# Cross attention of a decoder: the softmax denominators as matmuls of ones over every tile of exps, instead of adds on GpSimd and VectorE ahead of them

## What is computed

```python
xn = layernorm(x, ...)                      # the context, 64 keys a batch, 192 wide
ln = layernorm(latents, ...)                # the 1024 tokens themselves, 256 wide
q  = ln @ Wq.T
kv = concatenate([xn @ Wkv.T, ln @ Wlkv.T], axis=1)
...                                         # 4 heads of 64; q and k normed per head
attn = where(full_mask, qn @ kn.T, -max)
attn = softmax(attn, axis=-1)               # over 1024 + 64 keys
out  = (attn @ v) -> (b, 1024, 256)
return out @ Wo.T + bo
```

## Time and profile before

| | |
|---|---|
| median of 3 runs | 1945.41 us (1944.75 to 1947.19) |
| the profiled execution | 1944.75 us, span 1943.0 us |
| busy over the span | TensorE 1688.1 us (87%), VectorE 941.2 (48%), ScalarE 625.1 (32%), GpSimd 119.4 (6%) |
| loop of the cross attention | about 423 to 700 us of the span |
| exps of the slots (line 878) | 64, 65.5 us |
| values (line 747), exps by v | 69.5 us busy |

### The profile page before, as it was taken

How to read it: one execution, slowest core, us unless ns; L and a number is a source line. 1 busy time by engine, 2 the same in 40 slices (tenths; PEclk the granted TensorE clock), 3 DMA queues, 4 the chain that set the end, 5 groups by cost and what they waited for, 6 DMA issues and landing times. The chain is left out here.

```text
span 1943.0 us, 19762 instructions
## 1 busy us (share of the span) xinstructions
PE 1688.1 (87%) x7458; PEld 955.6 (49%) x7458; DVE 941.2 (48%) x1490; ACT 625.1 (32%) x1024; POOL 119.4 (6%) x92
## 2 busy tenths in 40 slices
PE   5796795989999958977799999778767999999998
PEld 3443442543222213333444544345553888888886
DVE  3404404567656541133587775355545536353542
ACT  2312322432232231114166666242242222221220
POOL 0000000001121200003500000000011000000000
PEclk8898897989999979988899999899968999999999
DMA  4001000000000000002724520000111022222211
GB/s 174 0 0 59 0 0 4 0 1 1 1 1 1 1 1 0 0 0 76 87 82 52 67 34 2 3 1 0 52 36 58 1 87 87 87 87 87 87 30 44
DMA packets 27693, 67.47 MB, mean 35 GB/s; under 512 B 3096, under 2 KB 14424, under 8 KB 25176
## 3 DMA queue, kind: packets, MB, share of 16 engines
q1 hardware_dynamic: 27608, 66.33, 12.5%
HBM read 57.80 MB, written 8.39 MB: 34 GB/s over the span
## 5 line engine op out<-in xcount | busy, mean ns | idle before, releaser
L1566 ACT ACTIVATE arena<-psum 128x512 f32<-128x512 f32 (+3 forms) x384 | 164.3, 499 | 123.6 <-PE psum L1470 91.6
L1606 DVE TENSOR_REDUCE b_mx<-psum 128x1 f32<-128x512 f32 (+3 forms) x304 | 181.5, 653 | 45.0 <-PE psum L1448 34.4
L2100 PE MATMUL psum<-m_wo,m_hidden 128*128 128x256 f32 (+1 forms) x704 | 153.4, 379 | 1.0 <-DVE arena L2303 1.0
L2198 ACT ACTIVATE m_gelu<-psum 128x512 f32<-128x512 f32 (+1 forms) x88 | 52.6, 598 | 305.1 <-PE psum L2086 305.1
L2100 PEld LDWEIGHTS psum<-m_wo,m_hidden 128*128 128x128 f32 (+1 forms) x704 | 133.3, 190 | 19.7 <-issue 1.2
L2086 PE MATMUL psum<-m_x_high,m_w_high 128*128 128x512 f32 (+1 forms) x352 | 139.9, 398 | 2.9 <-issue 2.9
L2086 PE MATMUL psum<-m_x_rest,m_w_high 128*128 128x512 f32 (+1 forms) x352 | 138.8, 394 | 0.0
L2086 PE MATMUL psum<-m_x_high,m_w_rest 128*128 128x512 f32 (+1 forms) x352 | 138.4, 393 | 0.0
L2322 DVE TENSOR_TENSOR m_hidden<-m_gelu,psum 128x512 f32<-128x512 f32 (+1 forms) x88 | 60.5, 688 | 139.8 <-PE psum L2086 139.8
L878 ACT ACTIVATE x_probs<-psum 128x1024 f32<-128x1024 f32 x64 | 65.5, 1024 | 179.4 <-PE psum L734 179.4
L954 DVE TENSOR_REDUCE x_mx<-psum 128x2 f32<-128x1024 f32 x64 | 77.4, 1222 | 83.6 <-PE psum L708 82.4
(11 more groups left out here) (372 smaller groups left out, 2730.8 us busy)
## 6 DMA issues: line engine op xcount, KB each, us to landing
m_w<-w SPq DMA_DIRECT2D x16, 1368.0 KB, 8.9
m_wo<-wo SPq DMA_DIRECT2D x8, 1280.0 KB
weights_sb<-weights SPq DMA_DIRECT2D x2, 2820.0 KB, 8.9
b_q_stack<-b_q_dram SPq DMA_DIRECT2D x36, 128.0 KB, 6.9
b_k_stack<-b_k_dram SPq DMA_DIRECT2D x36, 128.0 KB, 7.4
weights_sb<-weights SPq DMA_DIRECT2D x1, 3328.0 KB, 13.0
b_q_dram<-b_q_parts SPq DMA_DIRECT2D x6, 512.0 KB, 3.3
b_k_dram<-b_k_parts SPq DMA_DIRECT2D x6, 512.0 KB, 4.4
```

What stands on the lines that cost most here:

```text
L1566: act.activation(probs[slot % RING][:, 0:n], score(slot)[:, 0:n], ACT.Exp, scale=SCALE).then_inc(s["expd"].sem)
L1606: dve.tensor_reduce(mx[:, part, qi, heads[0]:heads[0] + nh], tile(("piece", p))[:, 0:nh * keys].rearrange("p (h n) -> p h n", n=keys), AX, ...
L2100: mm = pe.matmul(bank[:, q * D:(q + 1) * D], hidden[0:H_N(h), h, (2 * i + q) * P:(2 * i + q + 1) * P], wo[0:H_N(h), h, :], start=(h == 0), ...
```

## The change

The adds on GpSimd and VectorE go, with `pool_sum`, `dve_sum` and `add_up`. TensorE sums each tile of exps itself: after `values` of the slots `kt` 1, 3, 5 and 7 it issues four matmuls with ones of 128x32 as stationary operand, two tiles by two heads, each into its own group of 32 partitions of `den_tile`; after `values` of slot 8 two more with 64 rows. The four groups hold partial sums (two for each head). `copy_out` now copies both banks (`psum[2]`, output and partial sums) to an `x_out` twice as wide. In slot 2 of the next step `spread_den` multiplies the copied partial sums by the constant `spread`, which has ones in four of its rows and so adds the two partial sums of a head and spreads them over its 64 rows. That result takes a place in the shared ring, from which `normalise` (now in slot 2 instead of 3) takes the reciprocal. `project` and `finish` move from slot 7 to slot 6. `exps` now waits only for the values (and the sums with them) that still read the tile.

```diff
+            if n >= 1 and kt == 2:
+                order.append(("den", n - 1))
-            if n >= 1 and kt == 7 and part_of(n - 1)[2] == FT - 1:
+            if n >= 1 and kt == 6 and part_of(n - 1)[2] == FT - 1:
                 order.append(("project", n - 1))
...
-    order.append(("project", STEPS - 1))
+    order += [("den", STEPS - 1), ("project", STEPS - 1)]
...
-        ones = sb("x_ones", [P, DH])
+        spread = sb("x_spread", [P, P])
+        ones = sb("x_ones", [P, 32])
...
-        out_sb = sb("x_out", [P, CH])
-        pool_sum = [sb(f"x_pool_sum{i}", [P, PAIR, CH]) for i in range(2)]
-        dve_sum = sb("x_dve_sum", [P, PAIR, CH])
+        out_sb = sb("x_out", [P, 2 * CH])
...
+                pool.memset(spread[:], 0.0)
...
-                for n in range(STEPS):
-                    if n >= 2:
-                        pool.wait_ge(*s["den"](n - 1))
-                    for kt in range(1, POOLED):
-                        slot = GROUPS * n + kt
-                        pool.wait_ge(*s["expd"](slot + 1))
-                        if kt > 1:
-                            pool.wait_ge(*s["pooled"]((POOLED - 1) * n + kt - 1))
-                        pool.tensor_tensor(pool_sum[n % 2][:], probs[(slot - 1) % RING][:] if kt == 1 else pool_sum[n % 2][:],
-                                           probs[slot % RING][:], ALU.add).then_inc(s["pooled"].sem)
+                pool.wait_ge(g["zeroed"].sem, 3)
+                pool.memset(spread[0:1, 0:DH], 1.0)
+                pool.memset(spread[32:33, DH:P], 1.0)
+                pool.memset(spread[64:65, 0:DH], 1.0)
+                pool.memset(spread[96:97, DH:P], 1.0).then_inc(g["consts"].sem)
...
+                    if kt % 2 == 1:
+                        for back in (1, 0):
+                            for h in range(PAIR):
+                                group = PAIR * (1 - back) + h
+                                mm = pe.matmul(den_tile[group * 32:(group + 1) * 32, :], ones[:], probs[(slot - back) % RING][:, h, :],
+                                               start=(kt == 1), stop=(back == 0 and kt == TT - 1))
+                    if kt == TT:
+                        for h in range(PAIR):
+                            mm = pe.matmul(den_tile[h * 32:(h + 1) * 32, :], ones[0:KEYS, :], probs[slot % RING][0:KEYS, h, :],
+                                           start=False, stop=True)
                     mm.then_inc(s["av"].sem)
 
-                def add_up(n):
-                    pe.wait_ge(*s["pooled"]((POOLED - 1) * (n + 1)))
-                    pe.wait_ge(*s["added"]((TT - POOLED) * (n + 1)))
-                    if n >= 1:
-                        pe.wait_ge(*s["den_inv"](n))
-                    for i, of in enumerate((pool_sum[n % 2], dve_sum)):
-                        for h in range(PAIR):
-                            mm = pe.matmul(den_tile[h * DH:(h + 1) * DH, :], ones[:], of[:, h, :], start=(i == 0), stop=(i == 1))
-                    mm.then_inc(s["den"].sem)
+                def spread_den(n):
+                    to = tile(("den", n))
+                    pe.wait_ge(*s["out_copied"](n + 1))
+                    pe.matmul(to[:, 0:CH], spread[:], out_sb[:, CH:2 * CH], start=True, stop=True).then_inc(s["made"].sem)
...
-                        m, of = divmod(slot - RING, GROUPS)
-                        act.wait_ge(*s["av"](slot - RING + 1))
-                        if of < POOLED:
-                            act.wait_ge(*s["pooled"]((POOLED - 1) * m + max(of, 1)))
-                        else:
-                            act.wait_ge(*s["added"]((TT - POOLED) * m + max(of - POOLED, 1)))
+                        act.wait_ge(*s["av"](slot - RING + 1 + (1 if (slot - RING) % GROUPS % 2 == 0 and (slot - RING) % GROUPS < TT else 0)))
...
-                    act.activation(out_sb[:], out_tile, ACT.Copy).then_inc(s["out_copied"].sem)
+                    act.activation(out_sb[:], c.psum[2][:], ACT.Copy).then_inc(s["out_copied"].sem)
...
-                def add(slot):
...
                 def normalise(n):
                     b, half, m = part_of(n)
-                    dve.wait_ge(*s["den"](n + 1))
-                    dve.reciprocal(den_inv[:], den_tile).then_inc(s["den_inv"].sem)
-                    dve.wait_ge(*s["den_inv"](n + 1))
-                    dve.wait_ge(*s["out_copied"](n + 1))
-                    dve.tensor_tensor(ot[b][:, m, half * CH:(half + 1) * CH], out_sb[:], den_inv[:], ALU.mult).then_inc(s["normed"].sem)
+                    dve.reciprocal(den_inv[:], tile(("den", n))[:, 0:CH]).then_inc(s["read"].sem)
+                    dve.wait_ge(*s["read"](nth["den", n] + 1))
+                    dve.tensor_tensor(ot[b][:, m, half * CH:(half + 1) * CH], out_sb[:, 0:CH], den_inv[:], ALU.mult).then_inc(s["normed"].sem)
...
-                        if n >= 1 and kt == 0:
-                            add(GROUPS * n - 1)
-                        if kt > POOLED + 1:
-                            add(GROUPS * n + kt - 1)
-                        if n >= 1 and kt == 3:
+                        if n >= 1 and kt == 2:
                             normalise(n - 1)
```

More of the change, by code:

```diff
@@ L570, in cross_attention_layer @@
                                        made=0, read=0, masked=0, ctx_max=0, negated=0, max_step=0, parts=0,
-                                       scored=0, expd=0, av=0, pooled=0, added=0, den=0, out_copied=0, den_inv=0, normed=0))
+                                       scored=0, expd=0, av=0, out_copied=0, den_inv=0, normed=0))
         g = signals(nc, ctx, "xc", dict(load=1, zeroed=1, consts=1, mean=1, cent=1, sq=1, var=1, log=1, rstd=1, scaled=1,
@@ L614, in cross_attention_layer @@
         units, out_tile, den_tile = c.psum[0], c.bank(4), c.bank(5)
-        POOLED = 4
         two_heads = lambda ap: ap.rearrange("p (h n) -> p h n", h=PAIR)
@@ L640, in _ @@
                 pool.memset(same_head[0:DH, 0:DH], 1.0 / DH)
-                pool.memset(same_head[DH:P, DH:P], 1.0 / DH).then_inc(g["consts"].sem)
-                for n in range(STEPS):
-                    if n >= 2:
-                        pool.wait_ge(*s["den"](n - 1))
-                    for kt in range(1, POOLED):
-                        slot = GROUPS * n + kt
-                        pool.wait_ge(*s["expd"](slot + 1))
-                        if kt > 1:
-                            pool.wait_ge(*s["pooled"]((POOLED - 1) * n + kt - 1))
-                        pool.tensor_tensor(pool_sum[n % 2][:], probs[(slot - 1) % RING][:] if kt == 1 else pool_sum[n % 2][:],
-                                           probs[slot % RING][:], ALU.add).then_inc(s["pooled"].sem)
+                pool.memset(same_head[DH:P, DH:P], 1.0 / DH).then_inc(g["zeroed"].sem)
+                pool.wait_ge(g["zeroed"].sem, 3)
[3 more added lines that the diff above has]
+                pool.memset(spread[96:97, DH:P], 1.0).then_inc(g["consts"].sem)
             @block.tensor
@@ L831, in _ @@
                     if n >= 1 and kt == 2:
-                        add_up(n - 1)
-                    if n >= 1 and kt == 7 and part_of(n - 1)[2] == FT - 1:
+                        spread_den(n - 1)
+                    if n >= 1 and kt == 6 and part_of(n - 1)[2] == FT - 1:
                         project(n - 1)
@@ L841, in _ @@
                 values(SLOTS - 1)
-                add_up(STEPS - 1)
+                spread_den(STEPS - 1)
                 project(STEPS - 1)
@@ L1089, in _ @@
                             keep_shift(n + 1)
-                add(SLOTS - 1)
                 normalise(STEPS - 1)
```

## The result

The changed kernel takes 1981.72 us (median of 4 runs, 1981.13 to 1983.76), the kernel before 1946.24 beside it: +35.5 us, ratio 1.0185 with a 95% interval of 1.0167 to 1.0203. The profiled execution took 1980.98, its span 1979.3.

The account below looks back on a forecast made before the run. TensorE bounds the stage (busy 32.16 of 33.00 us). Rounds +32.3, last step's slots +0.8, +0.3 and +2.3, spread -4.0, copy +3.0, wait -1.3, tail +1.1: +34.5, so 1979.5 us; range 1974 to 1987.

Parts of the forecast that it names:

- The round: Each burst of sum matmuls after values, 5 per step, 40 in all: 0.95 us each, bounds 0.86 and 1.01.
- Spread for `add_up`: Slot 2: `add_up`'s 1.72 us go, one spread matmul of 1.05 comes; -0.67 a step, -4.0 in steps 1 to 6.
- The copy: Output copy twice as wide, 1.02 us for 0.59, on TensorE's path: +0.43 seven times, +3.0 us.
- The covered wait: Where steps meet, TensorE's two shift-copy waits go, with the add gone and the round after values 7 covering: -1.3 us.
- The move of the projection: Projection from slot 7 to 6, its inputs ready before it and its VectorE reader moving too: costs nothing.
- The clock: TensorE's granted clock: no term in the sum; extra or missing falls at the borders put at 1.6 us each.
- The tail: From the start of the last values 8 to the projection: 8.57 us instead of 7.51, +1.1.
- A: Rival: clock falls behind the 1.27 us copy wait at each step's start, six times, +9.6 us, 1989; chance 0.14.
- B: Rival: the four column groups run two and two, a round is 1.72 us, +31 us, 2010; chance 0.03.
- C: Rival: rounds cost TensorE nothing, -2.9 us, 1942.5; faster only below 0.07 us a round; chance 0.03 together with D.
- D: Rival: whole kernel within 0.2% (3.9 us), needing rounds of at most 0.17 us; chance 0.03 together with C.
- E: Rival: VectorE lags and piece 5 waits the whole reciprocal for its ring place, 7 x 3.4 = +24 us, 2003; chance 0.03.

Follow-up runs that it names:

- wide copy: Kernel before with only its output copy widened to 1024 columns; 1949.16 us, ratio 1.0010 to the kernel before, stage +4.1 us.
- one pair: Kernel before with copy early, VectorE's chain starting from GpSimd's sum (one add more), so one pair of sum matmuls instead of two; 1935.05 us, ratio 0.9943.
- 64-wide kernel: Changed kernel with 128x64 sum matmuls in two column groups instead of four, without the spread matmul; 1996.55 us, ratio 1.0259 to the kernel before.
- copy early: Output copy moved ahead of slot 1's exp: changed kernel 1968.95 us (ratio 1.0115), kernel before 1934.37 us (0.9941).
- rounds twice: Changed kernel with the rounds after values 3, 5 and 7 issued two times; 2005.90 us, ratio 1.0303 to the kernel before.
- before, no adds: Kernel before without any adds on GpSimd and VectorE, the sum tiles holding constants; 1943.48 us, ratio 0.9985 to the kernel before.
- after, fewer rounds: Changed kernel without the rounds after values 3, 5 and 7; 1958.83 us, ratio 1.0073 to the kernel before.

## Why the prediction was right

**The bound.** That the stage is TensorE's and that the adds stand on almost nobody's path held: without any adds the kernel gains about 2 us. What was put on TensorE came out at the end, but for the 0.2 us a slot that the last step had idle.

**The round**, the main term, was 0.99 instead of 0.95, inside the bounds 0.86 and 1.01. By the lengths of the slots that is +1.2 over the 40 rounds: slots 4 and 6 grew by 0.99, slot 0 by 0.98, slot 8 by 0.96, and the last step's slots 4 and 6 by 0.81 for 0.77. The row that described it best was the upper bound, a pair alone in its shape: a round is always alone in its shape.

**Spread for `add_up`** was 1.06 for 1.05 and right. **The copy** was right, +0.43 seven times, and is confirmed alone by the wide copy. **The covered wait** was right at 1.3, but its reason was half wrong: the add that went was enough, the round had no part in it. Another 0.5 us of small waits went with the adds, 0.4 of it in slot 6 of step 0; the sum has no term for them.

**The move of the projection**, which I put at nothing, costs 0.2 three times. Slot 7 without pieces has an idle moment in which TensorE waits for the exp. Before, the projection stood in that slot in every other step and hid it. Now it stands in slot 6, as the timeline shows:

```profile
603.03 3.70 PE L768 MATMUL psum<-weights_sb 128*128 128x512 f32 x8
606.66 1.08 PE L743 MATMUL psum<-x_probs,arena 128*64 128x512 f32 x4
...
608.98 1.13 PE L730 MATMUL psum<-arena 64*128 64x512 f32 x4
610.04 1.08 PE L743 MATMUL psum<-x_probs,arena 128*64 128x512 f32 x4
611.24 0.40 PE L725 MATMUL psum<-x_shift_t,x_ones 2*64 2x512 bf16 x2
```

From the start of slot 7's values to the next instruction it is 1.20 us (610.04 to 611.24) where a covered pair takes 1.01. That is most of why the steps that follow each other here grew by 4.6 and 4.9 us in turn (output copy to output copy: 34.94 to 39.82 with a projection, 31.56 to 36.20 without).

**The clock** was left out of the sum, rightly on the whole and luckily in one place. The fall in the last step of the earlier trace rows did not come back, -1.6. So the stage's +34.3 against a forecast of +34.5 is closer than the terms were: +1.2 for the rounds and +0.6 for the projection were missing, and -1.6 for that fall and -0.5 for the small waits made up for them. Such a near hit is luck; that the time lies between the bounds for rounds of 0.86 and 1.01 is not.

**The tail** was +1.1 and right.

**The rivals.** A (the clock falls behind the wait of 1.27) did not happen here: in five executions with six such waits each it fell behind none of the 30. But it was near: behind the one wait of 1.57 us (one pair) it fell, and at 2.19 us three times of six. B is ruled out by the bursts themselves and by the 64-wide kernel. C and D would have needed rounds of 0.07 and 0.17 us. E (the ring) did not happen: no piece waits for the reciprocal.

**Total.** The rest of the 35.5 us between the medians is not in the stage. In the profiled executions 2.1 us lie ahead of it, in code that is the same; the prediction had nothing for that. It does not come with the change: the burst of 5.84 us took 3.70 in the changed kernel with the copy early, and 5.63 in the kernel before with the copy early. Why it takes the one time or the other no run shows.

## What to carry to other kernels

Before work is taken off an engine, ask which wait of the bound engine ends on it. Here GpSimd and VectorE did 95 us of adds under TensorE's cover, and taking all of them away is worth about 2 us, while summing on TensorE costs 40 times about 1 us. The same reading pointed to what could be won: the one wait of the bound engine that came back in every step was for a copy of 0.59 us that stood behind an exp in its queue, and moving it by one place gained 8.7 us in the stage (12 in the median, ratio 0.9941), a quarter of what the whole change cost there. And a burst of matmuls that is alone in its tile shape is priced as such, not as one more of a row.

## What the runs showed of the hardware

- Four 128x32 matmuls of 512 fp32 columns in four column groups cost 0.86 us together (the second round of rounds twice), as much as two of 128x64 in two groups; a round that stands alone between bursts of another shape costs 0.13 more (0.99).
- Whether TensorE's clock falls from 2.4 to 1.2 GHz behind a wait is not decided by the wait's length alone. In steps 1 to 6 it fell behind 1.27 us never (30 waits), behind 1.57 the one time that this wait occurred (one pair), behind 2.19 three times of six. Behind the wait ahead of the last step's values 0 it fell at 1.70 us in one execution and not in another (before, no adds), and at 2.13 us in three (rounds twice, 64 wide, wide copy) and not in two (after, fewer rounds). What decides between them no run here shows. A fall of 3.4 us cost 1.6 to 1.7, one of 6.8 us about 3.
- The same code, behind the changed stage, took 304.6 to 305.0 us in nine executions and 308.4 or 308.5 in two, and no run shows why. So differences of 2 to 3 us in the whole kernel are best read from the stage.
